# A four-layer kernel: the opening work of layer 0 as one program by chunks, layer 1's small products in four lanes, and clears moved

## The chip, the cores and the metric

The kernel runs on one core of a Trainium2 chip. The metric is the device time of one execution in microseconds; lower is better. The core has five engines with a program each: PE (TensorE, matrix products), DVE (VectorE), ACT (ScalarE), POOL (GpSimd) and SP (SyncE, which here only starts transfers). They meet through semaphores. PE's clock is granted at one of two levels, 1.2 or 2.4 GHz; a profile gives the granted level as a share of full speed.

## The reference

An activation `x` of 2 x 1024 tokens with 256 features goes through four residual layers, each a "conditioning" step and a feed-forward step. The change touches the first conditioning step and layer 1.

```python
# layer 0, conditioning: a demodulated product, w scaled per batch by the condition y
w1 = weight * y                        # per batch, with y / sqrt(256)
out = x @ (w1 / sqrt(sum(w1 ** 2) + 1e-8))
# layer 1, conditioning: attention with a query that is shared by all rows of a batch
q, k, v = x @ Wq.T, x @ Wk.T, x @ Wv.T          # 16 heads of 16
a = (Wt @ cond) . q                             # one weight per head and row
qmod = einsum('bhs,bhse->bhe', a, q)
scores = where(mask, qmod . k / sqrt(e), min); o = softmax(scores) @ v; out = o @ Wo.T
# layer 1, feed-forward: 16 experts' q, k, v and output projections,
# each weighted per token by a gating softmax rw; causal attention; out = sum_e rw_e * (ao @ o_proj_e)
```

Since the query of layer 1 does not depend on the row, all rows of a batch get the same attention result wherever all rows of `mask` are alike. Then the feed-forward part too is one row per batch, which is added to all 1024 tokens. The kernel tests this at run time and has a short branch for it, which the inputs take.

## The kernel before

Tokens are kept in SBUF as `xtok` (128 partitions x 16 tiles x 256) and, turned, as features `fx`/`fc` (128 x 2 halves x 2048 tokens). Both lie in one large tile, `sb_big` in the profile, as does `acc`. PE turns a block by a product with `ident`. The program is a row of *blocks*: in each, every engine has its own list, and the next block begins when all five have finished. After a group of blocks come two barriers of all engines and the release of semaphores (`with_own_semaphores`, line 2565).

Layer 0 opens with four blocks. `stage_load` (lines 105 to 162) loads `x` in one transfer of 2 MB, the condition, biases and router weights; ACT then waits for all of them and starts the clears of the scratch table `sorted_in` (39 tiles of 128 rows, 5.11 MB, three transfers), which only layer 2 reads. `stage_to_features` (L173, L181, L187) turns `x` in 32 transposes. `stage_l0_cond` loads its weight (L229), squares and folds it on DVE (L237, L240), gets the norm (L264), and does 16 products of 128x128 by 128x512 (L273), which DVE scales out of PSUM (L252). `stage_to_tokens` turns the result back in 32 transposes (L198, L206, L212). `half_l0` follows: router, shared expert, 32 routed experts whose weights are streamed by SP, results added. Its first PE rows are L298.

Layer 1, on this input, has four blocks. `stage_l1_project` (lines 1836 to 1940) loads the mask and the five weights, takes the query of every token (L1871, 16 products), copies it out (L1898), multiplies it by a block-diagonal condition (L1880) and sums over tokens on DVE (L1923), which gives `qmod` and then `U` (L1890). DVE meanwhile compares the mask's 8 tiles with its first row, one compare and one sum per tile (L1907, L1909). The count `differ` decides the branch. `stage_l1_same_rows` scores both batches in 16 output rows (L2428), softmax, a weighted sum of tokens (L2442), three small products; then a block `stage_l1_gating` with its own loads; then a block with the 16 experts' `v` projection (L2523: 32 products with two columns), output projection (L2529: 32 more), and the addition of the row to `fx` (L2553) and `xtok` (L2558). Layer 2's first rows follow.

Every fp32 product shows as two records in the profile, a transpose as one.

## Time and profile before

| | |
|---|---|
| median of 3 runs | 1822.16 us (1815.49 to 1824.17) |
| profiled execution | 1827.07 us, of it 1825.3 us span |
| mean granted PE clock | 0.905 |
| PE, DVE, ACT, POOL busy | 84%, 56%, 36%, 23% |
| span to the first row of `half_l0` on PE | 60.35 us |
| layer 1, first DVE row to layer 2's first ACT row | 371.93 to 497.84 us |

The span is cut below into the stages that the change touches and the rest. A profiled execution is one sample; its time lies a little above the highest of the three timed runs.

### The profile page before, as it was taken

How to read it: one execution, taken by the hardware profiler on the slowest of the kernel's cores; microseconds unless marked ns; L12 is line 12 of the kernel's file. 1: busy time of each engine (PE TensorE's matmuls, PEld its weight loads, DVE VectorE, ACT ScalarE, POOL GpSimd, SP SyncE). 2: the span in 40 equal slices, each digit the busy share in tenths (PEclk: the TensorE clock that was granted, in tenths of full speed). 3: DMA queues.
4: the chain of work that ended last, by engine and by line, in shares of the span. 5: the costliest groups of instructions: out<-in, count | busy, mean ns of one | idle time of the engine just before them, and what ended most of it. 6: DMA issues, size and time to landing. Idle time of an engine off the chain costs nothing. (4 is left out here: it accounts for less than half of the span.)

```text
span 1825.3 us, 26214 instructions
## 1 busy us (share of the span) xinstructions
PE 1533.0 (84%) x8442; PEld 1164.3 (64%) x8442; DVE 1013.2 (56%) x1801; ACT 661.3 (36%) x981; POOL 428.0 (23%) x364
## 2 busy tenths in 40 slices
PE   3788878866689999879799999999988699848993
PEld 2553323733668778768688888888776577725662
DVE  2737767452263435473577777776546133536675
ACT  1337767211032333242455555554323133211110
POOL 0412222000034241001033334342003334023321
PEclk9989989886579999989899999999997699959996
DMA  6328981213031334024022221300303232245733
GB/s 200 137 93 331 364 310 58 84 55 93 23 137 62 103 101 150 1 81 162 3 90 99 94 97 57 134 28 14 133 1 130 101 99 79 95 142 203 265 109 107
DMA packets 82585, 211.11 MB, mean 116 GB/s; under 512 B 10561, under 2 KB 57426, under 8 KB 74258
## 3 DMA queue, kind: packets, MB, share of 16 engines
q1 hardware_dynamic: 61568, 160.98, 24.8%
q0 software_dynamic: 15840, 43.27, 7.0%
q10 hardware_dynamic: 5042, 5.11, 0.8%
q8 instruction: 78, 1.28, 0.3%
q14 instruction: 57, 0.47, 0.1%
HBM read 164.90 MB, written 44.43 MB: 115 GB/s over the span
## 5 line engine op out<-in xcount | busy, mean ns | idle before, releaser
L593 POOL DMA_INDIRECT results<-sb_big,sb_s_out_row x63 | 132.8, 2108 | 465.1 <-ACT sb_big L824 303.1
L898 DVE TENSOR_TENSOR sb_h_split<-sb_big,sb_h_split 128x2048 fp32r<-128x2048 f32 x78 | 178.5, 2290 | 87.9 <-ACT sb_h_split L893 87.9
L893 ACT CAST sb_h_split<-sb_big 128x2048 fp32r x78 | 146.6, 1903 | 41.9 <-issue 40.6
L789 PE MATMUL ps<-sb_big,sb_e_hT 128*128 x624 | 141.0, 379 | 1.1 <-DVE sb_e_hT L942 1.1
L282 PE MATMUL ps<-sb_h_split 128*128 128x512 f32 x312 | 133.6, 428 | 9.6 <-DVE sb_h_split L917 6.8
L1031 DVE COPY sb_g_space<-sb_big 128x1024 f32 x168 | 108.4, 699 | 47.0 <-DMA sb_big<-in_l_routed 24.9
L1031 ACT COPY sb_g_space<-sb_big 128x1024 f32 x120 | 118.7, 1050 | 41.7 <-DMA sb_big<-in_l_routed 32.4
L1421 POOL DMA_INDIRECT sorted_in<-sb_big,sb_p_slots x64 | 70.6, 1104 | 260.6 <-DVE sb_p_slots L1247 216.8
L789 PEld LDWEIGHTS ps<-sb_big,sb_e_hT 128*128 128x128 f32 x624 | 118.2, 190 | 18.5 <-issue 1.3
L282 PE MATMUL ps<-sb_g_split,sb_g_ws 128*128 128x512 f32 x256 | 109.6, 428 | 23.3 <-DVE sb_g_product L461 15.7
L284 PE MATMUL ps<-sb_h_split 128*128 128x512 f32 x312 | 124.1, 398 | 0.0
L283 PE MATMUL ps<-sb_h_split 128*128 128x512 f32 x312 | 123.9, 397 | 0.0
L1069 PE MATMUL ps<-sb_g_space,sb_e_rT 128*32 128x512 f32 x768 | 99.9, 640 | 18.3 <-ACT sb_g_space L1031 8.5
L555 POOL DMA_INDIRECT results<-sb_big,sb_p_out_row x78 | 77.6, 995 | 145.3 <-DVE sb_big L704 144.6
L283 PE MATMUL ps<-sb_g_split,sb_g_ws 128*128 128x512 f32 x256 | 107.3, 419 | 0.0
L284 PE MATMUL ps<-sb_g_split,sb_g_ws 128*128 128x512 f32 x256 | 106.5, 416 | 0.0
L282 PE MATMUL ps<-sb_g_ws,sb_g_split 128*128 128x256 f32 x256 | 79.6, 311 | 26.1 <-DVE sb_g_split L467 18.5
L582 POOL DMA_INDIRECT sb_big<-by_token,sb_s_in_row x63 | 64.5, 1025 | 153.0 <-DVE sb_s_out_row L1294 134.4
L436 ACT ACTIVATE sb_g_sg<-ps 128x512 f32<-128x512 f32 x64 | 38.2, 598 | 157.0 <-PE ps L284 108.8
L636 PE MATMUL ps<-sb_big,sb_x_rT 128*128 x312 | 87.5, 403 | 4.1 <-ACT sb_x_rT L681 4.0
L461 DVE TENSOR_TENSOR sb_g_product<-sb_g_sg,ps 128x512 f32<-128x512 f32 x64 | 43.8, 685 | 70.8 <-ACT sb_g_sg L436 54.2
L656 PE MATMUL ps<-sb_big,sb_x_hT 128*128 x312 | 82.1, 386 | 0.0
(416 smaller groups left out, 3318.6 us busy)
## 6 DMA issues: line engine op xcount, KB each, us to landing
sb_big<-in_l_routed SPq DMA_DIRECT2D x32, 1024.0 KB
sb_big<-in_l2f_routed SPq DMA_DIRECT2D x8, 3072.0 KB, 11.1
sb_e_wring<-in_l_experts SPq DMA_DIRECT2D x16, 1408.0 KB
sb_big<-in_l_routed SPq DMA_DIRECT2D x32, 512.0 KB
sb_big<-results SPq DMA_DIRECT2D x32, 512.0 KB, 7.4
sb_big<-sorted_in SPq DMA_DIRECT2D x18, 512.0 KB
by_token<-sb_big SPq DMA_DIRECT2D x12, 512.0 KB, 3.6
sorted_in<-sb_big ACTq DMA_DIRECT2D x2, 2048.0 KB
```

The lines of the kernel that those rows point to most:

```text
L282: pe.matmul(to, w[0], x[0], start=start, stop=False)
L283: pe.matmul(to, w[0], x[1], start=False, stop=False)
L284: return pe.matmul(to, w[1], x[0], start=False, stop=stop)
L555: pool.indirect_dma_start(out=results, out_offset=bass.IndirectOffsetOnAxis(ap=places.out_row[:, j:j + 1], axis=0), in_=self.tile(j), in_o ...
L593: pool.indirect_dma_start(out=results, out_offset=bass.IndirectOffsetOnAxis(ap=places.out_row[:, j:j + 1], axis=0), in_=self.tile(j), in_o ...
L636: last = pe.matmul(psum[:, j % 2, 0:self.NF * P], self.rT[:, j % 2, k * P:(k + 1) * P], self.w[:, e, k * self.NF * P:(k + 1) * self.NF * P ...
L656: last = pe.matmul(psum[:, 2 + j % 2, 0:D], self.hT[:, j % 2, f * P:(f + 1) * P], self.w[:, e, lo:lo + D].rearrange("p s n -> p (s n)"), s ...
L789: last = pe.matmul(psum[:, 7, 0:D], self.hT[:, f // TPC, f % TPC * P:(f % TPC + 1) * P], self.weight(place, 2 * KD * self.F + f * D, D), s ...
L893: act.copy(self.own[part][:, 0, :], self.raw(e, part)).then_inc(self.own_high[part], 1)
L898: dve.tensor_tensor(self.own[part][:, 1, :], self.raw(e, part), self.own[part][:, 0, :], ALU.subtract).then_inc(self.own_low[part], 1)
L1031: last = copy(self.own[part][:, g, :], here.rearrange("p s n -> p (s n)"))
L1069: last = pe.matmul(psum[g * W:(g + 1) * W, 2 * part + u % 2, :], self.rT[:, r % 2, k, g * W:(g + 1) * W], self.own[part][:, g, lo:lo + FU] ...
```

## The change

The layer-0 opening becomes one block, `layer0_front`. `x` comes in four chunks of 512 tokens with a semaphore each, behind the condition and the weight. PE turns chunk 0 and 1, then for each chunk does the product, turns the chunk two ahead, and turns back the one before; DVE and ACT copy and scale in the same order. ACT clears only row 0 of `by_token`.

Layer 1's weights (now six, with a second layout of `Wq`) and the mask, viewed as 32-bit words, are loaded by SP at the end of `half_l0` into free parts of `sb_big`. `stage_l1_project` does not form the query of every token any more: it folds condition and `Wq` into 32 columns `V`, multiplies all tokens by them with four column groups of PE side by side (*lanes*: chunk g goes to partitions 32g to 32g+31), turns the result, and takes the weighted sum of tokens in the same manner. DVE compares the mask in three instructions over 2048 words per partition. SP clears `sorted_in` in this block, out of a zero tile that POOL makes; layer 2's POOL waits for it (`swept`). `stage_l1_same_rows` is one block with its loads at its head, the gating inside it, and the two expert projections in lanes (8 products of 32x512, 16 of 32x256). ACT takes half of the addition to `fx`. The branch for masks that differ is nearly unchanged.

```diff
-        def stage_load():
...
-                    sp.dma_start(xtok, a["x"].rearrange("(i p) d -> p i d", p=P)).then_inc(loaded, 16)
...
-                    act.wait_ge(loaded, 16 * 9)
-                    for lo in range(0, SLOT_TILES2, NT):
-                        hi = min(SLOT_TILES2, lo + NT)
-                        act.dma_start(sorted_in[lo * P:hi * P, :].rearrange("(i p) d -> p i d", p=P),
-                                      acc[:, 0:hi - lo, :]).then_inc(zeroed, 16)
-                    act.dma_start(by_token[0:1, :], acc[0:1, 0, :]).then_inc(zeroed, 16)
...
+        def layer0_front():
...
+                        sp.dma_start(condT[:], a["condT"]).then_inc(cond_in, 16)
+                        sp.dma_start(w[:], a["l0_cond_w"]).then_inc(w_in, 16)
+                        for c in range(NCH):
+                            sp.dma_start(xtok[:, c * TPC:(c + 1) * TPC, :],
+                                         a["x"][c * CH:(c + 1) * CH, :].rearrange("(i p) d -> p i d", p=P)).then_inc(x_in[c], 16)
+                        sp.dma_start(wr0[:], a["l0_gate"]).then_inc(loaded, 16)
+                        sp.dma_start(wbuf[:], unit_data["l0"]).then_inc(unit_in["l0"], 16)
...
+                        turn(0)
+                        pe.wait_ge(folded, 1)
+                        turn(1)
+                        for c in range(NCH):
+                            product(c)
+                            if c + 2 < NCH:
+                                turn(c + 2)
+                            if c >= 1:
+                                turn_back(c - 1)
+                        turn_back(NCH - 1)
...
+                        act.wait_ge(cleared, 1)
+                        act.dma_start(by_token[0:1, :], acc[0:1, 0, :]).then_inc(zeroed, 16)
...
+                        for c in range(NCH):
+                            scale(c)
+                            if c + 2 < NCH:
+                                to_features(c + 2)
+                            if c >= 1:
+                                to_tokens(c - 1)
+                        to_tokens(NCH - 1)
...
+                        sp.dma_start(l1_weights, a["l1_w"]).then_inc(l1_in, 16)
+                        sp.dma_start(l1_words[:, 0:TPB, :], a["mask_words"].rearrange("(i p) s -> p i s", p=P)
+                                     ).then_inc(l1_mask, 16)
+                        sp.dma_start(l1_words[:, TPB, :], a["mask_words"][0, :].partition_broadcast(P)).then_inc(l1_mask, 16)
...
-                        pool.wait_ge(zeroed, 16 * (1 + -(-SLOT_TILES2 // NT)))
+                        pool.wait_ge(zeroed, 16)
...
+                        if n == 2:
+                            pool.wait_ge(swept, 16 * 3)
...
-            stage_to_features("a0", xtok, fx)
-            stage_l0_cond()
-            stage_to_tokens("b0", fc, ctok)
+            layer0_front()
...
+        def in_lanes(pe, to, w, bank):
+
+            for k in range(KD):
+                for g in range(NCH):
+                    last = pe.matmul(psum[g * EQ:(g + 1) * EQ, bank, :], w[:, k, :], fx[:, k, g * CH:(g + 1) * CH],
+                                     start=(k == 0), stop=(k == KD - 1))
+            last.then_inc(to, 1)
...
+        def lanes_times_rows(pe, to, turned, bank):
+
+            for q in range(TPC):
+                for g in range(NCH):
+                    last = pe.matmul(psum[g * EQ:(g + 1) * EQ, bank, 0:D], turned[:, q, g * EQ:(g + 1) * EQ],
+                                     xtok[:, g * TPC + q, :], start=(q == 0), stop=(q == TPC - 1))
+            last.then_inc(to, 1)
...
+                        for lo in range(0, SLOT_TILES2, NT):
+                            n = min(SLOT_TILES2 - lo, NT)
+                            sp.dma_start(sorted_in[lo * P:(lo + n) * P, :].rearrange("(i p) d -> p i d", p=P),
+                                         zero[:].unsqueeze(1).to_broadcast([P, n, D])).then_inc(swept, 16)
...
+                        pe.wait_ge(vc, 1)
+                        in_lanes(pe, ad, V, 0)
+                        pe.wait_ge(ac, 1)
+                        turn_lanes(pe, atd, lanes, TPC, 1)
+                        pe.wait_ge(atc, 1)
+                        lanes_times_rows(pe, rd, aT, 2)
+                        pe.wait_ge(rc, 1)
+                        turn_lanes(pe, rtd, r, KD, 3)
...
-                            dve.tensor_tensor(ne[:], m8[:, i, :], m1[:], ALU.not_equal).then_inc(counted, 1)
-                            dve.wait_ge(counted, 2 * i + 1)
-                            dve.tensor_reduce(cnt[:, i:i + 1], ne[:], AX_X, ALU.add).then_inc(counted, 1)
...
+                    for g in range(NCH):
+                        sp.dma_start(m1[g * EQ:(g + 1) * EQ, :],
+                                     a["mask"][0, g % 2 * CH:(g % 2 + 1) * CH].partition_broadcast(EQ)).then_inc(masked, 16)
+                    sp.dma_start(simc[:, :, 0:E], a["l1_sim"]).then_inc(simmed, 16)
+                    sp.dma_start(gb[:], a["l1_gates"].partition_broadcast(P)).then_inc(simmed, 16)
+                    for k in range(KD):
+                        sp.dma_start(wv[:, :, k, :], a["l1_qkv"][:, :, k, 2 * H1:3 * H1]).then_inc(wloaded, 16)
+                    sp.dma_start(wo[:], a["l1_o"]).then_inc(wloaded, 16)
...
-            stage_l1_gating(rw, shared=cb)
...
-                        for e in range(E1):
-                            for k in range(KD):
-                                last = pe.matmul(psum[:, 0, e * B:(e + 1) * B], wv[:, e, k, :], c[:, k, :],
-                                                 start=(k == 0), stop=(k == KD - 1))
-                        last.then_inc(vd, 1)
...
+                    pe.wait_ge(wloaded, 48)
+                    for k in range(KD):
+                        for g in range(4):
+                            last = pe.matmul(psum[g * EQ:(g + 1) * EQ, 6, :], c32[:, k, :], wv[:, 4 * g:4 * g + 4, k, :],
+                                             start=(k == 0), stop=(k == KD - 1))
+                    last.then_inc(vd, 1)
+                    pe.wait_ge(vsd, 1)
+                    pe.matmul(psum[:, 5, 256:256 + B], vs[:], sel[:], start=True, stop=True).then_inc(vtd, 1)
...
+                    pe.wait_ge(avd, 2)
+                    for n in range(4):
+                        for g in range(4):
+                            last = pe.matmul(psum[g * EQ:(g + 1) * EQ, 7, 0:D], av[:, 4 * g + n, :], wo[:, 4 * g + n, :],
+                                             start=(n == 0), stop=(n == 3))
+                    last.then_inc(outd, 1)
...
+                    act.wait_ge(simmed, 32)
+                    act.activation(gb[:], gb[:], ACT.Sigmoid).then_inc(rooted, 1)
+                    act.wait_ge(maxd, 1)
+                    act.activation(pr[:], pr[:], ACT.Exp, bias=mx[:, 0:1], accum_out=sums[:, 0:1]).then_inc(expd, 1)
...
-        with_own_semaphores(stage_load)
...
```

PE's rows at the start of the program, before: `sb_big` holds `x` and its turned copy, `sb_l0c_wb` the folded weights; a branch row is the step into the next block.

```order
L173 MATMUL ps<-sb_ident,sb_big 128x128 x32
L167 UNCONDITIONAL_BRANCH
L259 UNCONDITIONAL_BRANCH
L264 MATMUL ps<-sb_l0c_ys,sb_l0c_w 128x2 x4
L273 MATMUL ps<-sb_big,sb_l0c_wb 128x512 x16
L226 UNCONDITIONAL_BRANCH
L192 UNCONDITIONAL_BRANCH
L198 MATMUL ps<-sb_ident,sb_big 128x128 x32
```

The same place in the changed program (L172 turns a chunk, L184 is the product, L196 turns it back):

```order
L203 MATMUL ps<-sb_l0c_ys,sb_l0c_w 128x2 x4
L172 MATMUL ps<-sb_ident,sb_big 128x128 x16
L184 MATMUL ps<-sb_big,sb_l0c_wb 128x512 x4
L172 MATMUL ps<-sb_ident,sb_big 128x128 x8
L184 MATMUL ps<-sb_big,sb_l0c_wb 128x512 x4
L172 MATMUL ps<-sb_ident,sb_big 128x128 x8
L196 MATMUL ps<-sb_ident,sb_big 128x128 x8
L184 MATMUL ps<-sb_big,sb_l0c_wb 128x512 x4
L196 MATMUL ps<-sb_ident,sb_big 128x128 x8
L184 MATMUL ps<-sb_big,sb_l0c_wb 128x512 x4
L196 MATMUL ps<-sb_ident,sb_big 128x128 x16
```

The 80 products and transposes and the norm are the same in number; the three steps between blocks are gone, and the norm stands first.

PE's rows in layer 1 before, first of the projection block, then of the last block of the short branch:

```order
L1863 MATMUL ps<-sb_condT,sb_l_w 128x2 x4
L1871 MATMUL ps<-sb_big,sb_l_w 128x512 x16
L1880 MATMUL ps<-sb_big,sb_l_bd 128x512 x8
L1884 MATMUL ps<-sb_l1p_cnt,sb_ones 1x8
L1890 MATMUL ps<-sb_l_qm,sb_l_w 128x16 x8
...
L2523 MATMUL ps<-sb_f_c,sb_f_wbuf 128x2 x32
L2529 MATMUL ps<-sb_f_av,sb_f_wbuf 128x2 x32
L2535 MATMUL ps<-sb_ident,sb_f_rowb 128x128 x4
```

And in the changed program (`V`, `aT`, `rb` lead to the query, `wv` and `wo` are the experts' weights):

```order
L1935 MATMUL ps<-sb_condT,sb_big 128x2 x4
L1941 MATMUL ps<-sb_l_tpm,sb_big 128x32 x4
L1867 MATMUL ps<-sb_big,sb_l_V 32x512 x8
L1882 MATMUL ps<-sb_ident,sb_l_lanes 128x128 x4
L1875 MATMUL ps<-sb_big,sb_l_aT 32x256 x16
L1882 MATMUL ps<-sb_ident,sb_l_r 128x128 x2
L1956 MATMUL ps<-sb_l_rb,sb_big 128x32 x4
L1963 MATMUL ps<-sb_l_qm,sb_big 128x32 x4
...
L2545 MATMUL ps<-sb_f_wv,sb_f_c 32x512 x8
L2549 MATMUL ps<-sb_f_sel,sb_f_vs 128x2
L2553 MATMUL ps<-sb_f_wo,sb_f_av 32x256 x16
L2558 MATMUL ps<-sb_f_sel,sb_f_rows 128x2 x2
```

The 24 wide products of the projection become 8 of a quarter of the width in output rows plus 16 short ones, and 64 two-column products of the experts become 24 in lanes.

## Rows read from the trace of the kernel before

**Rows 1.** The first line of the page.
```profile
span 1825.3 us, 26214 instructions
```

**Rows 2.** Busy time by stage: opening, layer 1's four blocks, the rest.
```profile
core 0: us, PE busy (x) PEld busy (x) DVE busy (x) ACT busy (x) POOL busy (x), PEclk, DMA share, GB/s
0.00:60.30 60.30, 27.60 (x104) 17.15 (x104) 18.17 (x32) 7.46 (x11) 2.25 (x15) 0.94 0.47 152
...
371.80:413.70 41.90, 27.38 (x74) 13.55 (x74) 27.41 (x46) 4.92 (x9) 0.71 (x3) 0.79 0.17 60
413.70:444.00 30.30, 25.81 (x92) 11.45 (x92) 6.16 (x18) 3.53 (x5) 0.07 (x1) 0.73 0.44 139
444.00:459.90 15.90, 4.45 (x20) 4.34 (x20) 6.02 (x32) 4.60 (x7) 0.00 (x0) 0.50 0.02 3
459.90:497.50 37.60, 28.72 (x132) 28.17 (x132) 8.38 (x12) 0.00 (x0) 0.00 (x0) 0.50 0.00 0
```

**Rows 3.** Timeline of the opening: start, duration, instruction, idle before it.
```profile
11.11 11.33 ACTq L127 DMA_DIRECT2D sorted_in<-sb_big  x3
...
25.78 5.81 PE L173 MATMUL ps<-sb_ident,sb_big 128*128 128x128 f32 x32 [25.78 <-PEq L2567]
...
35.01 0.69 DVE L237 TENSOR_TENSOR sb_l0c_w<-sb_l0c_w 128x512 f32<-128x512 f32 x1 [2.13 <-DMA sb_l0c_w<-in_l_cond_w]
...
37.61 17.05 PE L273 MATMUL ps<-sb_big,sb_l0c_wb 128*128 128x512 f32 x32 [0.80 <-DVE sb_l0c_d L246]
...
55.75 3.69 PE L198 MATMUL ps<-sb_ident,sb_big 128*128 128x128 f32 x32 [1.09 <-PEq L226]
...
60.35 1.92 PE L298 MATMUL ps<-sb_big,sb_wr 128*32 128x512 f32 x16 [0.92 <-PEq L191]
```

**Rows 4.** Transfers issued in the opening: KB, and us from issue to landing.
```profile
sb_big<-in_x SPq DMA_DIRECT2D x1, 2048.0 KB, 8.4
```

**Rows 5.** DVE's groups in the opening: busy us, mean ns, idle before.
```profile
L252 DVE TENSOR_SCALAR sb_big<-ps,sb_l0c_d 128x512 f32<-128x512 f32 x8 | 6.0, 751 | 12.0 <-PE ps L273 12.0
...
L206 DVE COPY sb_big<-ps 128x512 f32<-128x512 f32 x4 | 2.8, 692 | 1.5 <-PE ps L198 1.5
```

**Rows 6.** Granted clock during L273 (columns of rows 2).
```profile
42.00:44.00 2.00, 2.00 (x4) 0.90 (x3) 0.23 (x1) 0.00 (x0) 0.00 (x0) 0.55 0.00 0
44.00:46.00 2.00, 2.00 (x6) 0.85 (x5) 0.75 (x1) 0.00 (x0) 0.00 (x0) 1.00 0.00 0
```

**Rows 7.** Granted clock in layer 1 (columns of rows 2).
```profile
371.80:389.00 17.20, 7.17 (x15) 4.08 (x16) 10.06 (x10) 0.59 (x1) 0.69 (x2) 0.51 0.41 145
389.00:411.00 22.00, 19.70 (x57) 9.06 (x56) 16.92 (x34) 4.10 (x7) 0.00 (x0) 1.00 0.00 1
```

**Rows 8.** Costliest groups of the projection block (columns of rows 5).
```profile
L1871 PE MATMUL ps<-sb_big,sb_l_w 128*128 128x512 f32 x32 | 16.5, 679 | 0.0
...
L1909 DVE TENSOR_REDUCE sb_l1p_cnt<-sb_l1p_ne 128x1 f32<-128x1024 f32 x8 | 9.8, 1220 | 0.3
...
L1863 PE MATMUL ps<-sb_condT,sb_l_w 128*128 128x2 f32 x8 | 1.9, 356 | 12.2 <-DMA sb_l_w<-in_l_w 12.2
```

**Rows 9.** Timeline of the gating block (columns of rows 3).
```profile
447.94 1.28 ACT L2141 ACT_TABLE_LOAD   x1
...
453.67 0.19 DVE L2165 TENSOR_TENSOR sb_g1s_L<-sb_g1s_L,sb_g1s_ns 128x32 f32<-128x32 f32 x1
453.90 0.19 DVE L2166 TENSOR_TENSOR sb_g1s_L<-sb_g1s_L,sb_g1s_gb 128x32 f32<-128x32 f32 x1
```

**Rows 10.** Transfers issued in layer 1 (columns of rows 4).
```profile
sb_g1s_gb<-in_l_gates SPq DMA_DIRECT2D x1, 8.0 KB, 3.1
```

**Rows 11.** Costliest groups of the last block of layer 1 (columns of rows 5).
```profile
L2529 PE MATMUL ps<-sb_f_av,sb_f_wbuf 128*128 128x2 f32 x64 | 13.8, 352 | 0.9 <-DVE sb_f_av L2546 0.9
...
L2558 DVE TENSOR_TENSOR sb_big<-sb_big,ps 128x2048 f32<-128x2048 f32 x2 | 4.5, 2280 | 0.0
```

**Rows 12.** Timeline of PE at the start of layer 2 (columns of rows 3).
```profile
501.56 3.41 PE L298 MATMUL ps<-sb_big,sb_wr2c 128*32 128x512 f32 x16
```

More of the change, by code:

```diff
@@ new lines, in lanes_times_rows, with turn_lanes @@
+        def lanes_times_rows(pe, to, turned, bank):
+            for q in range(TPC):
+                for g in range(NCH):
+                    last = pe.matmul(psum[g * EQ:(g + 1) * EQ, bank, 0:D], turned[:, q, g * EQ:(g + 1) * EQ],
+                                     xtok[:, g * TPC + q, :], start=(q == 0), stop=(q == TPC - 1))
+            last.then_inc(to, 1)
+        def turn_lanes(pe, to, lanes, n, bank):
+            for q in range(n):
+                last = pe.transpose(psum[:, bank, q * P:(q + 1) * P], lanes[:, q * P:(q + 1) * P], ident[:])
+            last.then_inc(to, 1)
@@ L1883, in _ @@
[L1883 to L1891 removed]
+                        pe.wait_ge(tpmd, 2)
@@ new lines, in _ @@
+                        for d in range(KD):
+                            for o in range(KD):
+                                last = pe.matmul(psum[:, 6, d * BH:(d + 1) * BH], w6[:, WQT, o, d * P:(d + 1) * P],
+                                                 tpm[:, o, :, :].rearrange("p b h -> p (b h)"),
+                                                 start=(o == 0), stop=(o == KD - 1))
+                        last.then_inc(vd, 1)
+                        pe.wait_ge(vc, 1)
+                        in_lanes(pe, ad, V, 0)
@@ L1892, in _ @@
+                        last.then_inc(qd, 1)
+                        pe.wait_ge(qmd, 2)
+                        for d in range(KD):
+                            for o in range(KD):
+                                last = pe.matmul(psum[:, 5, d * BH:(d + 1) * BH], w6[:, WK, o, d * P:(d + 1) * P],
+                                                 qm[:, o, :, :].rearrange("p b h -> p (b h)"),
+                                                 start=(o == 0), stop=(o == KD - 1))
                         last.then_inc(ud, 1)
+                        pe.wait_ge(counted, 1)
@@ L1894, in _ @@
+                        pe.matmul(psum[0:1, 7, 64:65], ones[:, 0:1], cnt[:], start=True, stop=True).then_inc(flagd, 1)
                     @block.scalar
                     def _(act):
-                        for n in range(8):
-                            act.wait_ge(qd, n + 1)
-                            act.copy(q[:, n // NCH, n % NCH * CH:(n % NCH + 1) * CH], psum[:, n % 4, :]).then_inc(qc, 1)
+                        act.wait_ge(ad, 1)
+                        act.copy(lanes[:], psum[:, 0, :]).then_inc(ac, 1)
@@ new lines, in stage_l1_same_rows @@
+            E, BH = E1, B * HEADS
+            wv = sb("f1_wv", [P, E, KD, H1], on=own)
+            wo = sb("f1_wo", [P, E, D], on=own)
+            m1 = sb("f1_m1", [P, CH], U8, on=own)
+            lim = sb("f1_lim", [P, CH], on=own)
+            pr = sb("f1_pr", [P, CH], on=own)
+            pT = sb("f1_pT", [P, TPC, P], on=own)
+            mx, sums = (sb("f1_" + n, [P, 1], on=own) for n in ("mx", "sums"))
+            spread = sb("f1_spread", [P, 2, P], on=own)
+            peak, total, share, tmp2 = (sb("f1_" + n, [P, B, 2, HEADS], on=own) for n in ("peak", "total", "share", "tmp2"))
@@ L2570, in layer1 @@
             with ExitStack() as own:
[L2571 removed]
+                w6 = l1_weights
                 U = sb("l1_U", [P, KD, B, HEADS], on=own)
```

804 lines of the change are left out of this document (420 added, 384 removed).

## The prediction, made before the changed kernel ran

> **What bounds the kernel now.** I read the page first: the span is 1825.3 us [rows 1], and its profiled execution took 1827.1 us. The chain that ended last covers only the last 1% of the span, so it says nothing about the places of this change. I then cut the span at the borders of the edited blocks and took the busy time of each stretch [rows 2]. The reader is to see that no engine is full in any of them. The opening takes 60.3 us and PE, the busiest engine, works 27.6 of it. Layer 1 runs from 371.8 to 497.5, in pieces of 41.9, 30.3, 15.9 and 37.6 us, 125.7 in all. DMA is idle in most of it (share 0.17, 0.44, 0.02, 0.00). These stretches are dependent chains, so what counts is the length of the chain, and an instruction off it is free.
>
> The timeline of the opening [rows 3] shows the chain. ACT issues three clears from 11.11 for 11.33 us, and PE's first transpose is at 25.78, only after them, although `x` landed 8.4 us after its issue at the start [rows 4]. Then come 5.81 us of transposes, 2.13 us of waiting for a weight that had no reason to come so late, 17.05 us of products, 3.69 us of transposes and, at 60.35, the router. The clears are on the path because the block ends only when ACT has issued them.
>
> In layer 1 PE waits 12.2 us for the weights before its first small product, then works 16.5 us on the query of every token, while DVE sums the mask in 8 pieces of 1.22 us beside as many compares [rows 8]. In the last block two sets of 64 records with two columns each take 13.8 us apiece, 27.6 of 37.6 us (one of them in [rows 11]): these pay for loading 128x128 weights, not for columns. The clock matters: at 0.51 of full speed in the first 17.2 us of the layer and 1.00 in the next 22 [rows 7], then 0.50 in the last two pieces [rows 2].
>
> **The opening, part by part.** The work on PE is the same; its place changes. Removed are the wait for clears and the steps between blocks. The condition and weight are first in SP's queue. I take 4 us for the weight, as its load made DVE wait about 2 us when issued alone [rows 3]. A 2 MB `x` took 8.4 us to land [rows 4]; if about 2 us of that is fixed, a quarter costs 1.6 and chunk 0 lands near 5.5, chunk 3 near 10. With no fixed part a quarter is 2.1 us and nothing below changes by more than 1 us. The norm is done at 5.7. Two chunks of transposes at the slow pace of the first ones (5.81 us for 32, 0.18 each) give 8.7. The 16 products I price as now, 17.05 us, which includes a slow start: the records before 44 us ran at a granted 0.55, those after at 1.00 [rows 6]. Between them stand 16 forward transposes and 16 backward ones at 0.115 each (3.69 for 32), 3.7 us. DVE's load per chunk is two scalings of 0.75 and two copies of 0.69 [rows 5], 2.9 us against 4 to 5 us of PE, so it is covered; with PE free it would be 11.5 us in all. At the end stand out one scaling, the copies of chunk 2 and 3 and the last 8 transposes, 0.75 + 0.69 + 0.92 + 0.69, plus 0.5 for a small DVE instruction and the step: 3.6. Sum 8.7 + 17.05 + 3.7 + 3.6 = 33.0 against 60.3, **27.3 us less**. Bounds: with a full clock throughout 3 us less; with the half clock throughout the products are 16 x 1.71 = 27.4 and the 56 later transposes 0.06 each dearer, so 13.7 more.
>
> What follows in layer 0 starts from the same state and keeps its length; its streamed weights are asked for at its own start, so they shift along. The shared expert's weights come behind `x`, 1.5 MB at the pace of `x`, near 16 us, 17 before use.
>
> **The prefetch.** SP issues 2.7 MB more behind the result loads at the end of layer 0. At the pace of `x` (2 MB in 8.4) they need 11 us, about 335 to 345, with some 25 us of product work left before layer 1. Cost nothing; without that cover up to 11 us.
>
> **Layer 1, projections.** After a first small product the engines take turns, PE's bursts being under 4 us. Now the clock came up only after some 6 us of continuous products and fell again in the waits [rows 7], so I price all at half clock: four small products in 1.9 us [rows 8], eight 32x512 in lanes in 3.4 us [rows 12] (1.92 at full clock [rows 3]), and sixteen 32x256 as the same columns. The chain: condition 1.9, masking 0.6, `V` 1.9 and copy 0.2, lanes 3.4, copy 0.6, four transposes 0.8, copy 0.7, lanes 3.4, copy, two transposes and DVE's halves 1.6, query 1.9, scaling 0.4, `U` 1.9 or beside it DVE's sum of 2048 words at 2 x 1.22 = 2.4, copies and flag 0.5. That is 20.3 us. DVE's word compare (2.3 us, as L2558's 2.28 for 2048 elements [rows 11]) lies behind the first lanes and its copies, the conversion (at most the same) behind the second. With the step to the next block, 1.7 us as now, 22.0 against 41.9: **19.9 less**. The clears are asked for at its head by SP: issue 11.3 us [rows 3], landing at most 5.11/2.1 x 8.4 = 20.4 us; that ends inside the block, and their reader is in layer 2. If they ran on, the next block's mask and gate loads would queue behind.
>
> **Layer 1, the rest.** Six small transfers go out first; the last is issued at 2.2 us and lands 3.1 later [rows 10], then sigmoid 0.2 and a table load of 1.28 [rows 9]: exp can start at 6.8, later than the scores (3.5) and their maximum (4.9). This wait is new, about 2 us; behind it on ACT stand exp and all that leads to the weighted sum, so PE and DVE wait too. Then exp 0.8, transposes and copy 1.5, spreading of maxima 1.1, lanes 3.4, copy, turn and weighting 1.6: 15.2. Three small products with their DVE parts, 2.3, 2.7 and 1.9: 22.1. Gating, 31 instructions at 0.23 from start to start [rows 9] and two trips to ACT, 8.2, which hides the first expert product (3.4 in place of 13.8): 30.3. Two DVE passes over 512, a tiny product and `av`, 2.4; second expert product 3.4 in place of 13.8; row 1.5; `fx` halved between DVE and ACT 1.4; `xtok` 4.5 as now: 43.5. With a step of 1.3, 44.8 against 83.8: **39.0 less**. The experts' weights land about 17 us in, needed at 22.
>
> Sum: 27.3 + 19.9 + 39.0 = 86.2 us. The profiled execution would take 1827.1 - 86.2 = 1740.9; it lay 4.9 above the median, so the median becomes **1736 us**.
>
> On the four lanes: 16 records took 3.41 us [rows 12], where at 0.85 a record they would be 13.7 in full width, a gain of 4.0. The Trainium skill (TensorE: Matmul & The Clock Gate, Measured speedup vs the span model) gives 3.07 for four row tiles and less than 3 for three column tiles. By that figure, an estimate, each of the five lane products would be 4.5 us, of them four on the path, and the time 1740. The row is of this very shape, so it decides.
>
> On the table switch: the load takes 1.28 us and the sequence needs nothing more in this trace [rows 9]. The Trainium skill (ScalarE: Activation LUTs, What ACT_TABLE_LOAD costs) adds a drain and gives 2.66 us for a switch; the sum would be 1737.
>
> **The rivals.**
> Half clock all through the opening (0.13). Chunks mix transposes into the products, and PE's first 32 transposes ran at 0.18 us, the later ones at 0.115. For it: the opening starts from idle and its bursts are broken. Against: the products alone are 3.4 us long with hardly a gap. By the bound above it costs 13.7 us: 1750 us. The same skill page (Part 4: PE-mode transpose) says that transposes do not count as work that raises the clock, which speaks for this case; it hangs on no row here.
> Clock up in layer 1 (0.10). Four small products 1.05 instead of 1.9, lanes 1.9 instead of 3.4: 13 us less, 1723. Against: every burst is under 4 us.
> Underpriced hand-overs or the clears colliding (0.14). If each of some 40 hand-overs cost 0.3 us more, or the clears took twice 15 us and pushed the mask loads 8 us back, the time is 1748.
> The opening gives nothing (0.03): if layer 0's streamed weights, not its start, set its end. They are issued at its own start, so this needs a limit that no row shows; 1763.
> Slower than before (0.02). PE leaves layer 1 at half clock, as now, where it recovered in 17 us of layer 2. If it stayed there, each microsecond of full PE work costs one more. It decides above 86 + 9 = 95 us of such work; layer 2 has over 200. One mechanism, and nothing in the trace shows it: 1832.
>
> **How the numbers follow.** My own sum has 0.58, with its own range 1727 to 1746. The rivals at 1750, 1748 and 1723 lie close by and are taken in, so the range is **1719 to 1758**; outside are the last two and tails. Half a per cent, 9 us, is about what a measurement tells from no change here (three runs lay 8.7 apart). Faster 0.96, same 0.02, slower 0.02.
>
> **What will show it.** PE's router rows should start near 33 us, the first transpose near 6, with at most 0.6 us between products and turns after the first. Layer 1 should be 67 us long from its first DVE row to layer 2, the projection block 20 and the other 43.5; mask loads should not be behind clears; lanes should take 3.4 us each at a granted 0.50. Wrong would be: a clock at 0.50 past 20 us, a clear still running at 394, an exp that starts later than 7 us into its block, or a stretch of layer 0 that grew by what the opening lost.

## The result, and the profile after

The changed kernel takes **1734.22 us** (median of four executions, 1731.22 to 1737.56); the kernel before, run beside it on the same chip, 1823.16 (1815.49 to 1827.36). The ratio is 0.9518, with a 95% interval from 0.9488 to 0.9547: 89 us less, where 86 were forecast. The profiled execution is the slowest of the four, 1737.56 us with a span of 1735.8.

Busy time by stage of the changed kernel, columns as in [rows 2]: opening, rest of layer 0, layer 1's two blocks, the step behind them, all the rest.

```profile
0.00:30.70 30.70, 24.32 (x105) 16.05 (x105) 14.92 (x32) 6.20 (x11) 2.25 (x15) 1.00 0.41 131
30.70:340.45 309.75, 249.48 (x2156) 137.68 (x2156) 191.42 (x310) 174.98 (x246) 70.65 (x64) 0.94 0.59 212
340.45:362.30 21.85, 15.35 (x88) 9.15 (x88) 8.32 (x17) 1.17 (x3) 0.96 (x4) 0.58 0.66 235
362.30:405.99 43.69, 24.60 (x142) 11.75 (x142) 20.65 (x72) 9.67 (x15) 0.60 (x2) 0.62 0.32 99
405.99:411.29 5.30, 0.00 (x0) 0.00 (x0) 0.00 (x0) 1.57 (x3) 0.00 (x0) 0.50 0.51 167
411.29:1735.80 1324.51, 1168.66 (x5864) 951.89 (x5864) 755.65 (x1351) 463.51 (x702) 351.67 (x282) 0.92 0.29 99
```

Against [rows 2] the opening is 29.7 us shorter (router's first row at 30.70, before at 60.35 [rows 3]), the projection block 20.0 (21.9 for 41.9), and the rest of layer 1 is one block of 43.7 us where three took 83.8 (to 497.5, and so with 1.3 us of the step behind them), with a step of 5.3 behind it. PE's share in the opening rose from 27.6 of 60.3 to 24.3 of 30.7. All this lies in the first 411 us.

PE's timeline in the opening after. The norm (L203) comes first; chunks then follow without a gap until the last turn:

```profile
4.80 1.87 PE L203 MATMUL ps<-sb_l0c_ys,sb_l0c_w 128*128 128x2 f32 x8 [4.80 <-DVE sb_l0c_w L252]
6.52 3.42 PE L172 MATMUL ps<-sb_ident,sb_big 128*128 128x128 f32 x16
9.78 3.60 PE L184 MATMUL ps<-sb_big,sb_l0c_wb 128*128 128x512 f32 x8
13.21 1.04 PE L172 MATMUL ps<-sb_ident,sb_big 128*128 128x128 f32 x8
...
28.71 1.06 PE L196 MATMUL ps<-sb_ident,sb_big 128*128 128x128 f32 x8 [0.66 <-DVE sb_big L275]
30.70 1.92 PE L335 MATMUL ps<-sb_big,sb_wr 128*32 128x512 f32 x16 [0.93 <-PEq L118]
```

PE's timeline in layer 1 after:

```profile
340.49 1.69 PE L1935 MATMUL ps<-sb_condT,sb_big 128*128 128x2 f32 x8 [2.42 <-PEq L2697]
...
345.05 3.64 PE L1867 MATMUL ps<-sb_big,sb_l_V 128*32 128x512 f32 x16 [0.32 <-DVE sb_l_V L1989]
...
384.43 3.64 PE L2545 MATMUL ps<-sb_f_wv,sb_f_c 128*32 128x512 f32 x16
393.97 0.59 PE L2549 MATMUL ps<-sb_f_sel,sb_f_vs 128*128 128x2 f32 x2 [5.90 <-DVE sb_f_vs L2676]
395.23 3.61 PE L2553 MATMUL ps<-sb_f_wo,sb_f_av 128*32 128x256 f32 x32 [0.67 <-DVE sb_f_av L2680]
...
411.29 0.41 PE L1415 MATMUL ps<-sb_condT,sb_wr2c 128*32 128x1 f32 x16 [10.37 <-issue]
```

Most of these products run at the half clock, as priced: the mean granted clock is 0.58 in the first block and 0.62 in the second. Where two experts' products of 13.8 us stood [rows 11], two of 3.64 and 3.61 stand, and behind the first PE still waits 5.90 us for the gating on DVE.

The new wait stands on ACT where it was forecast. Its timeline after:

```profile
367.83 0.22 ACT L2566 ACTIVATE sb_f_gb<-sb_f_gb 128x16 f32<-128x16 f32 x1 [4.46 <-DMA sb_f_gb<-in_l_gates]
368.06 1.28 ACT L2568 ACT_TABLE_LOAD   x1
369.36 0.72 ACT L2568 ACTIVATE sb_f_pr<-sb_f_pr,sb_f_mx 128x512 f32<-128x512 f32 x1
```

The exp's maximum was ready at 367.18 and the exp starts at 369.36, 7.06 us into its block: 2.2 us of waiting for the gates' load, the sigmoid and the table.

### The profile page after: what moved, and what is told of

Same layout as the page of the kernel before. It is cut to its first block and busy times, and to the rows that moved or that the text cites. A ratio compares the mean times of both kernels' runs of the same rounds, so it can differ in the third digit from the quotient of the medians.

```text
span 1735.8 us, 25954 instructions
## 1 busy us (share of the span) xinstructions
PE 1482.4 (85%) x8354; PEld 1126.5 (65%) x8354; DVE 991.0 (57%) x1782; ACT 657.1 (38%) x977; POOL 426.1 (25%) x366
## 5 line engine op out<-in xcount | busy, mean ns | idle before, releaser
L1106 PE MATMUL ps<-sb_g_space,sb_e_rT 128*32 128x512 f32 x768 | 95.7, 616 | 21.2 <-ACT sb_g_space L1068 9.6
L319 PE MATMUL ps<-sb_g_ws,sb_g_split 128*128 128x256 f32 x256 | 78.5, 307 | 25.2 <-DVE sb_g_split L504 14.5
## 6 DMA issues: line engine op xcount, KB each, us to landing
sb_big<-in_l2f_routed SPq DMA_DIRECT2D x8, 3072.0 KB, 10.5
```

The source lines that it names most:

```text
L319: pe.matmul(to, w[0], x[0], start=start, stop=False)
L1106: last = pe.matmul(psum[g * W:(g + 1) * W, 2 * part + u % 2, :], self.rT[:, r % 2, k, g * W:(g + 1) * W], self.own[part][:, g, lo:lo + FU] ...
```

## The experiments

Twelve kernels ran. Two yardsticks serve for all, and each profile is one sample. "Rows" is the start of the router's first row on PE, 30.70 in the changed kernel. "Layer 1" runs from the end of layer 0's last turn on PE to layer 2's first row on PE: 338.07 to 411.29, **73.2 us**, in the changed kernel. Code that no run altered varies by itself: with the same opening, "rows" lay at 30.7 to 32.4 in nine profiles, and the part after layer 1 lasted 1318.9 to 1325.3 us in the same nine. So medians some 5 us apart say little, and the trace decides. Layer 1 varies too. In the runs 1, 3 and 4 below its products are those of the changed kernel, and it lasted 75.6, 75.0 and 75.2 us, not 73.2: small products that took 1.08 and 1.05 us in the changed kernel's profile took 1.91 and 1.87 there, about twice as long. A difference from 73.2 is therefore uncertain by some 2 us, and where that matters the rows of the edited place are given.

**1. The old opening without its clears.** It separates the two halves of the opening's gain.

```diff
-            layer0_front()
+            stage_to_features("a0", xtok, fx)
+            stage_l0_cond()
+            stage_to_tokens("b0", fc, ctok)
...
+        with_own_semaphores(stage_load)
```

`stage_load` is as before, but without the three transfers into `sorted_in`.

> The changed kernel with the old four-block opening put back, but without the clears of the sorted rows in it (they stay in layer 1). Theory 1 (the clears' issue alone held the old opening for about 13.4 us of the 29.7 gained, from the clears' issue of 11.3 us and the wait behind it; work by chunks gives the other 16.3): the router's rows start at about 30.7 + 16.3 = 47 us and the time is 1734 + 16 = 1750. Rival 1 (nearly all of the gain was the clears; chunks only move work about): 1737 or less. Rival 2 (the clears ran hidden behind the loads, chunks gave it all): 1764.

Measured: 1754.17 us, ratio 0.9619 [0.9593, 0.9645]. PE's timeline of this run:

```profile
12.09 6.42 PE L356 MATMUL ps<-sb_ident,sb_big 128*128 128x128 f32 x32 [12.09 <-PEq L2845]
22.69 1.87 PE L447 MATMUL ps<-sb_l0c_ys,sb_l0c_w 128*128 128x2 f32 x8 [4.18 <-DVE sb_l0c_w L420]
25.36 16.95 PE L456 MATMUL ps<-sb_big,sb_l0c_wb 128*128 128x512 f32 x32 [0.80 <-DVE sb_l0c_d L429]
43.40 3.69 PE L381 MATMUL ps<-sb_ident,sb_big 128*128 128x128 f32 x32 [1.09 <-PEq L409]
48.01 1.49 PE L481 MATMUL ps<-sb_big,sb_wr 128*32 128x512 f32 x12 [0.92 <-PEq L374]
```

Rows at 48.01: the clears' place was worth 60.35 - 48.01 = **12.3 us**, the new order of the work 48.01 - 30.70 = **17.3 us**. Theory 1 holds, both rivals fall. The 17.3 are not the chunks' alone: PE's wait of 4.18 us before the norm, the steps between blocks and the slow first products went at the same time, and no run parts these.

**2. The new opening alone**, in the kernel before, with the clears on SyncE behind the opening's loads.

> The kernel before with the new opening alone: layer 1 as it was, and the clears issued by SyncE at the end of the opening's own list. Theory 1 (the parts add up, and the clears cost nothing behind the loads): 1823 less 29.7 less about 1.6 of layer 0 = 1792, router's rows from 30.7 us. Rival 1 (the clears on SyncE's queue hold the opening's end or its x loads): the rows start later than 31, by up to the clears' issue of 8 to 11 us, and the time is 1793 to 1803. Rival 2 (part of the 29.7 is only got together with layer 1's change): above 1800 with the rows at 30.7.

Measured: 1793.02 us, ratio 0.9834 [0.9808, 0.9860]; rows at 32.11. That is 29 us less than the kernel before, and its opening is 28.2 shorter (32.11 for 60.35). Both lie at the near edge of rival 1, but rows at 32.11 are within the 30.7 to 32.4 of the profiles without these clears, so it isn't borne out. The parts add up: the opening's gain needs nothing from layer 1.

**3. and 4. Where the clears stand.** In the changed kernel they go back into the opening, once on SyncE behind its loads, once on ScalarE ahead of its copies.

```diff
...
+                        sp.wait_ge(swiped, 1)
+                        for lo in range(0, SLOT_TILES2, NT):
+                            n = min(SLOT_TILES2 - lo, NT)
+                            sp.dma_start(sorted_in[lo * P:(lo + n) * P, :].rearrange("(i p) d -> p i d", p=P),
+                                         zero_rows[:].unsqueeze(1).to_broadcast([P, n, D])).then_inc(swept, 16)
                         sp.wait_ge(loaded, 16 * 7)
+                        sp.wait_ge(swept, 16 * 3)
...
```

> The changed kernel with the clears back in the opening, behind SyncE's loads. Theory 1 (what matters is only that the clears are off the queue that the products wait for; their place is free): 1734, within 2. Rival 1 (the clears' writes slow x and the weights' landings): the first rows of the router later than 30.7 by 1 to 5, 1736 to 1739. Rival 2 (their place in layer 1 cost something there): up to 2 faster, seen in a shorter projection block than 21.9.

> The changed kernel with the clears issued by ScalarE at the head of its list in the opening, ahead of its copies. Theory 1 (an issue on the engine that copies holds those copies): ScalarE's first copy, which now follows the transposes at about 8 to 9 us, comes after the issue of 8 to 11 us that starts at about 1, so 2 to 5 us late, and the opening ends as much later: 1736 to 1739. Rival 1 (the queue drains them in the background, hidden): 1734. Rival 2 (as costly as in the kernel before): 1745 or more.

On SyncE: 1737.71 us, ratio 0.9520 [0.9488, 0.9553], rows at 31.72. No difference from the changed kernel that can be told; PE's first products took 4.42 us in it, where the changed kernel's took 3.60, and in other profiles of the same opening they took 3.60 to 4.91, so this is most likely not the clears' doing. By its number and its rows this run would also fit rival 1; against that rival stands that `x` was asked for in 2.08 us in both and that the first transpose started at 6.39, in the changed kernel at 6.52. Rival 2 finds nothing either: the block in layer 1 that lost the clears was not shorter.

On ScalarE: 1754.64 us, ratio 0.9614 [0.9584, 0.9645], rows at 46.26, 14.5 late against SyncE's. ScalarE's timeline shows why:

```profile
1.15 13.67 ACTq L226 DMA_DIRECT2D sorted_in<-sb_l0c_zero  x3
14.87 6.52 ACTq L229 DMA_DIRECT2D by_token<-sb_big  x1
21.41 1.28 ACT L231 ACT_TABLE_LOAD   x1 [21.41 <-issue]
22.71 0.21 ACT L231 ACTIVATE sb_l0c_d<-sb_l0c_d 128x4 f32<-128x4 f32 x1
22.82 1.06 ACT L235 COPY sb_big<-ps 128x512 f32<-128x512 f32 x2
```

Rival 2 holds: I had counted the clears' issue of 11 us and left out the small transfer behind them. That one took 0.48 us in the changed kernel and 6.52 here, in line behind the clears, and the square root and all copies stand behind it. PE waited 8.78 us for the copy at 22.82. The clears also slowed the loads beside them: SyncE took 5.56 us to ask for `x` in place of 2.08, and the first transpose started at 9.94, but PE had turned both chunks by 14.75, well ahead of that copy. The two runs differ in the engine and in the place (ahead of the loads and copies, or behind the loads); the clears at the head of SyncE's list were not tried.

**5. No prefetch.** Layer 1's weights and the mask's words are loaded at the head of the projection block by the same three instructions.

> The changed kernel with layer 1's weights and the mask's words loaded at the head of the projection block, as before, and not in layer 0. Theory 1 (the weights' load stands ahead of everything in the block): the block grows from 21.9 by the load's issue and landing of 9 to 10.5 us less the start that it had anyway, so 1734 + 9 = 1743. Rival 1 (the half clock or the waits of the block hide part): 1738. Rival 2 (it gives nothing in layer 0 either way but also frees transfers there, .35 to .20 of the queue's share): layer 0 shorter by about 1, 1742.

Measured: 1742.59 us, ratio 0.9542 [0.9512, 0.9573]; layer 1 is 79.4 us, 6.2 more. The three loads stand ahead of the clears in SyncE's list. PE's timeline:

```profile
346.96 1.87 PE L1935 MATMUL ps<-sb_condT,sb_big 128*128 128x2 f32 x8 [8.81 <-DMA sb_big<-in_l_w]
```

8.81 us of waiting where the step to the block costs 2.42 anyway: the prefetch is worth **6.4 us**. I had expected 9, taking the landing times of 10.5 us that these transfers have behind layer 0's result loads; on an idle queue the weights landed 6.4 us after their issue. Theory 1's mechanism holds with a smaller price.

**6. The mask compared in bytes.** The 16 instructions of before, at the head of VectorE's list, in place of the three on words.

```diff
...
+                        dve.wait_ge(mloaded, 32)
+                        for i in range(TPB):
+                            if i:
+                                dve.wait_ge(counted, 2 * i)
+                            dve.tensor_tensor(ne[:], m8[:, i, :], m1[:], ALU.not_equal).then_inc(counted, 1)
+                            dve.wait_ge(counted, 2 * i + 1)
+                            dve.tensor_reduce(cnt[:, i:i + 1], ne[:], AX_X, ALU.add).then_inc(counted, 1)
                         dve.wait_ge(tpd, 1)
...
```

> The changed kernel with the mask compared as before by 16 instructions on bytes at the head of VectorE's list, and the rest of layer 1 new. Theory 1 (the count of about 16 instructions, eight pairs of some 1.6 us, stands ahead of VectorE's small copies that each product now waits for): the first product's copy comes about 13 us late, block 35, time 1747. Rival 1 (it is hidden behind the lanes' products as the one comparison is): 1736 or less. Rival 2 (only the flag comes late, at the block's end): 1738 to 1742.

Measured: 1762.48 us, ratio 0.9644 [0.9609, 0.9680]; layer 1 is 97.9 us, **24.7 more**, about twice what theory 1 expected. VectorE's groups between the block's start and its first copy:

```profile
L1990 DVE TENSOR_TENSOR sb_l1p_ne<-sb_l1p_m 128x1024 f32<-128x1024 uint8 x8 | 9.8, 1225 | 7.0 <-DMA sb_l1p_m<-in_mask 6.8
L1992 DVE TENSOR_REDUCE sb_l1p_cnt<-sb_l1p_ne 128x1 f32<-128x1024 f32 x8 | 9.8, 1220 | 0.3
```

Each pair costs 2.5 us, not 1.6, and the bytes' load adds 6.8 of waiting: 26.4, and PE's second product waited 25.66 for VectorE. The words, by contrast, are loaded in layer 0, cost 2.28, 1.22 and 2.28 us, and lie beside lanes and copies. In the kernel before this same compare lay beside 16.5 us of products [rows 8]; it ended at 398.8 there, and the last of those products at 400.0. With them gone it would be the bound of the block. The short chain and a compare off its path are one change. The run alters size and place together; 16 small instructions spread between the copies were not tried.

**7. and 8. The experts' products without lanes.** The v product, then the output product, as 32 separate products with two columns again.

```diff
...
-                    for n in range(4):
-                        for g in range(4):
-                            last = pe.matmul(psum[g * EQ:(g + 1) * EQ, 7, 0:D], av[:, 4 * g + n, :], wo[:, 4 * g + n, :],
-                                             start=(n == 0), stop=(n == 3))
+                    for f in range(KD):
+                        for e in range(E):
+                            last = pe.matmul(psum[:, 7, f * B:(f + 1) * B], wo[:, e, f * P:(f + 1) * P], av[:, e, 0:B],
+                                             start=(e == 0), stop=(e == E - 1))
...
```

> The changed kernel with the v product of the block of equal rows as 32 separate products again, without lanes. Theory 1 (its 13.8 us at half clock start at 384.4 beside the gating chain that ends at 392.2; about 6 us stick out, less some 2 us of lane sums on VectorE and TensorE that it doesn't need): 1734 + 4 = 1738. Rival 1 (hidden behind the gating): 1732 to 1734. Rival 2 (the busier TensorE comes to full clock by itself, product 7 us): 1732.

> The changed kernel with the output product of the block of equal rows as 32 separate products again, with the old broadcast and transposes behind it. Theory 1 (32 products of about 0.42 at half clock, 13.5, for 3.6, everything waits for it; the copy of rows and the products behind it, 2.2, against a broadcast and transposes of 2.7): 1734 + 10 = 1744. Rival 1 (the clock is full by then, as in the kernel before, where its output product took 4.5): 1734 to 1736. Which of the two holds tells how much of the lanes' gain is the lanes' own.

The v product: 1739.03 us, ratio 0.9526 [0.9506, 0.9545], layer 1 78.2 us, 5.0 more. The output product: 1746.33 us, ratio 0.9571 [0.9548, 0.9594], layer 1 84.2 us, 11.0 more. PE's timeline of the first:

```profile
388.10 13.79 PE L2545 MATMUL ps<-sb_f_c,sb_f_wv 128*128 128x2 f32 x64
402.88 3.64 PE L2551 MATMUL ps<-sb_f_wo,sb_f_av 128*32 128x256 f32 x32 [0.99 <-DVE sb_f_av L2671]
```

And of the second:

```profile
394.37 13.81 PE L2553 MATMUL ps<-sb_f_av,sb_f_wo 128*128 128x2 f32 x64 [0.67 <-DVE sb_f_av L2677]
```

From the start of the v product to that of the output product are 14.8 us, with lanes 10.8 (384.43 to 395.23; 10.8 also in run 1). So these lanes save 4.0 us, because the gating hides the rest; the same lanes in the output product, which nothing hides, save 13.81 - 3.61 = 10.2. Theory 1 holds in both. The second expectation's rival rests on a wrong figure: in the kernel before the output product took 13.8 us [rows 11], at a granted 0.50, and not 4.5.

**9. and 10. TensorE's waits filled.** 83 products of 128 by 128 (the expectation's 74 is a miscount) into an unused place, from layer 0's last turns to layer 1's end, each set sized to the wait that it stands ahead of; then the same with transposes of as much time.

```diff
+        def keep(pe, n, bank):
+            for i in range(n):
+                pe.matmul(psum[:, bank, 384:512], ones[:], ident[:], start=True, stop=True)
...
+                        keep(pe, 3, 5)
                         pe.wait_ge(ac, 1)
```

> The changed kernel with TensorE's waits from the last turns of layer 0 to the end of layer 1 filled with 74 products of 128 by 128 into an unused place of PSUM. Theory 1 (the half clock between 340 and 412 is what an often waiting TensorE gets; with its waits filled it keeps full clock): granted clock above 0.9 there, lanes' products 1.9 in place of 3.6, the two blocks shorter by 8 to 12: 1722 to 1727. Rival 1 (the clock stays half: small or narrow operations don't hold it): each wait is overrun by up to 0.4, 1737 to 1742. Rival 2 (clock full, but the fillers overrun the waits as much as it gains): 1732 to 1735.

> The same as the run with filling products, with transposes of as much time as fillers (5 for each 3 products). Theory 1 (a transpose holds the clock as a product does; in the opening products were at full clock behind 16 transposes): as the run with products, clock above 0.9, 1722 to 1728. Rival 1 (only products count, as the Trainium skill has it, in TensorE: Matmul & The Clock Gate): clock about 0.5 as without fillers, 1736 to 1742.

With products: 1727.60 us, ratio 0.9467 [0.9437, 0.9497], layer 1 67.1 us, 6.2 less than in the changed kernel. With transposes: 1728.82 us, ratio 0.9475 [0.9449, 0.9500], layer 1 65.0 us, 8.2 less. Windows of the run with products:

```profile
344.00:348.00 4.00, 4.00 (x20) 1.20 (x19) 2.42 (x2) 0.00 (x0) 0.00 (x0) 0.50 1.09 386
348.00:361.00 13.00, 9.95 (x88) 7.72 (x84) 5.28 (x10) 1.25 (x3) 0.09 (x2) 0.89 0.65 231
361.00:364.00 3.00, 2.92 (x16) 0.61 (x16) 0.00 (x0) 0.99 (x1) 0.52 (x2) 0.54 0.09 22
364.00:380.00 16.00, 13.32 (x119) 10.70 (x116) 6.46 (x29) 4.23 (x7) 0.00 (x0) 1.00 0.86 265
380.00:384.00 4.00, 3.79 (x20) 0.97 (x20) 2.86 (x17) 1.59 (x3) 0.00 (x0) 0.60 0.01 4
384.00:395.00 11.00, 10.26 (x96) 8.53 (x96) 6.42 (x25) 1.48 (x3) 0.00 (x0) 0.99 0.00 0
```

And of the run with transposes:

```profile
357.00:360.50 3.50, 3.50 (x16) 0.57 (x16) 0.00 (x0) 0.86 (x1) 0.39 (x1) 0.50 0.09 23
360.50:375.00 14.50, 12.06 (x108) 9.24 (x104) 6.46 (x29) 4.23 (x7) 0.00 (x0) 0.96 0.94 290
375.00:380.00 5.00, 5.00 (x25) 1.98 (x25) 2.78 (x16) 1.59 (x3) 0.00 (x0) 0.52 0.02 7
380.00:391.00 11.00, 10.15 (x88) 8.15 (x88) 6.41 (x25) 1.41 (x3) 0.00 (x0) 0.91 0.00 0
```

The seventh number is the granted clock. In the long stretches of chained work it is now 0.89 to 1.00 with either filler, and the 32x256 lanes took 1.93 us in place of 3.61. The changed kernel had 0.56 from 340.45 to 356, 0.50 from 362.3 to 378 and 0.65 from 382.5 to 405, with short stretches of 0.93 and 0.88 between. The rival of the second run falls with it: with transposes as fillers the clock stayed up as with products. The Trainium skill (TensorE: Matmul & The Clock Gate, Part 4: PE-mode transpose) says that they don't count; this trace disagrees, with 0.96 between 360.5 and 375 where the same work without fillers (362.3 to 378) had 0.50. Still the clock was at 0.50 to 0.60 in the lanes of 32x512, the first and the later one of the second block too, though TensorE was busy nearly all the time (4.00 of 4.00 us in the first): ahead of them stand small products of 2 to 32 columns, or the step between blocks. Why it fell there no run shows. So the gain in layer 1 is 6 to 8 us against the changed kernel's own profile, up to 11 against the 75.6 of run 1, and not 13 throughout. The 2 us between the two fillers are within what layer 1 varies by.

**11. The gates early.** The sigmoid, an idle exp that brings the table in, and the loads of mask lanes, similarities and gates move to the projection block.

```diff
                         act.copy(r[:], psum[:, 2, 0:D]).then_inc(rc, 1)
+                        act.wait_ge(simmed, 32)
+                        act.activation(gb[:], gb[:], ACT.Sigmoid)
+                        act.activation(idle[:], ones[0:1, 0:1], ACT.Exp)
```

> The changed kernel with the sigmoid of the gates, an idle exp behind it, and the loads of the mask's lanes, the similarities and the gates moved from the block of equal rows to the projection block. Theory 1 (the exp at 7.06 us into the block waits 2.2 us for the sigmoid and the table's load, nothing else is late there): exp at 4.9, time less 2.2: 1732. Rival 1 (the table is loaded anew at the exp in any case): less 0.9 or nothing. Rival 2 (another wait takes its place, the spread products' or the mask's): less 0 to 1, 1733 to 1734.

Measured: 1732.49 us, ratio 0.9496 [0.9464, 0.9527]; layer 1 71.8 us, 1.5 less, which is within its own variation. ScalarE's timeline has both table loads in the block before and none at the exp:

```profile
358.16 1.28 ACT L1984 ACT_TABLE_LOAD   x1
359.45 0.22 ACT L1984 ACTIVATE sb_f_gb<-sb_f_gb 128x16 f32<-128x16 f32 x1
359.67 1.28 ACT L1985 ACT_TABLE_LOAD   x1
...
371.21 0.72 ACT L2570 ACTIVATE sb_f_pr<-sb_f_pr,sb_f_mx 128x512 f32<-128x512 f32 x1 [10.04 <-DVEq L2593]
```

From the start of the scores' lanes to the transposes behind the exp are 5.4 us (366.64 to 372.08), in the changed kernel 7.8 (362.46 to 370.22), in the runs 1, 3 and 4 7.5 to 7.7: the wait of about 2.2 us is won. The time of the whole kernel can't tell 2 us, so this rests on the rows.

**12. Both together**: the filling products and the early gates.

> Filling products and the early gates together. Theory 1 (they add): 10 and 2.2, 1722; with the lanes' product faster the early exp is worth up to 4: 1720. Rival 1 (the fillers stay at half clock and cost): 1735 to 1740.

Measured: 1729.91 us, ratio 0.9476 [0.9451, 0.9500]; layer 1 64.1 us, 9.1 less than in the changed kernel and 3.0 less than with the fillers alone. From the scores' lanes to the transposes behind the exp are 6.6 us, with filling products alone 8.7, so the early gates are worth 2.1 here too: the two add in these rows (theory 1, which had put the sum at 12). The medians don't show it, 1729.91 against 1727.60 with products alone. The three versions with fillers are the fastest here, by their ratios 0.4 to 0.5% under the changed kernel, but their intervals touch its own. That they beat it rests on the shorter layer 1 in each trace, 64.1 to 67.1 us against 73.2 to 75.6.

**What was not run.** No run puts back the query of every token, or the three blocks of the rest of layer 1 with their steps. The prefetch (6.4 of the projection block's 20) and the experts' lanes (14.2 of the rest's 39) are priced by experiments; what is left in each, about 14 and 24 us, is read from the traces before and after.

## Why the prediction was right

**The opening** (27.3 forecast, 29.7 measured). The mechanism was right: clears off the path 12.3, the new order of the work 17.3. One term was mis-sized: "the 16 products I price as now, 17.05 us, which includes a slow start". They took 4 x 3.60 = 14.4. Against that the first products began at 9.78 where 8.7 was reckoned. The slow start belongs to the old order, where PE idles before its products; in the old opening without clears they took 16.95 again, at a granted 0.50 from 25 to 31 us. Here transposes stand right ahead of them. Other profiles of the same opening show up to 1.3 us of it. Behind an idle of 8.78 us, with the clears on ScalarE, the first products took 5.40. The rival of a half clock all through the opening does not hold: four of its products took 3.60 us, and at the half clock the prediction reckons 1.71 for each. The profile's own reading can't settle it: it is 1.00 from the start, though the norm took 1.87 us, while eight records of the same shape in layer 1 took 1.84 at a granted 0.50 (run 3) and 1.02 at 1.00 (run 9).

**The clears** (issue 11.3, inside the block). SyncE issued them from 340.79 for 7.83 us, where 11.3 was reckoned, and from 356 the DMA share is 0.01; the mask's loads are issued at 362.4. The half of that rival that rests on a collision falls. On SyncE they cost nothing that can be told in either place.

**The prefetch** (0, or up to 11 without cover). It cost layer 0 nothing that can be told: its remainder took 309.8 us, before 311.5, and from "rows" to the last turn it was 304.9 to 309.1 in eight profiles with it and 305.8 in the one without. It saves 6.4.

**The projections** (22.0 forecast, 21.9 measured). The small products took 1.69, 1.92, 1.08 and 1.92, lanes 3.64 and 3.36; PE's six waits for DVE and ACT up to the query 0.32 to 0.92. The half clock held, but for 2 us at 356 to 358, where it was 0.93. That the total fits to 0.1 us is luck: in five other profiles with the same products (runs 1, 3, 4, 7 and 8) the block lasted 23.5 to 23.8 us from its first product to the next block's, and 22.0 here (22.1 in run 5). The price of the compare (2.3) and that it lies behind the lanes were right; what it is worth I had not worked out, and the sixth run puts it at some 25 in this kernel (25.66 us of waiting where 0.63 is usual).

**The rest of layer 1** (block 43.5, then a step of 1.3; measured 43.7 and 5.3). Exp was forecast at 6.8 and came at 7.06, just past the 7 that was named as a sign of being wrong. The cause was the forecast's own, the gates' load, the sigmoid and the table; the maximum was ready at 4.88, as reckoned. The forecast's step ends at 497.5 [rows 2], but PE's first row lies later in both kernels: at 501.32 before, 5.1 us behind DVE's last row, and 5.3 behind it now. So 0.2 us was lost there. By the measure of the prediction, first DVE row to layer 2, the layer took 69.2 us to ACT's first row (340.54 to 409.72) and not 67: that row lies 3.7 us behind DVE's last one, before it lay 1.6 behind. Lanes: 13.8 us became 3.64 and 3.61 at the half clock, a gain of 3.8. By the Trainium skill's 3.07 for four row tiles (TensorE: Matmul & The Clock Gate, Measured speedup vs the span model), an estimate, they would have taken 4.5; the trace has less. The table load took 1.28 us and the exp began 0.02 behind it; the further drain that the Trainium skill gives (ScalarE: Activation LUTs, What ACT_TABLE_LOAD costs) is not in this trace.

**The clock in layer 1.** The rival at 1723 asked for a full clock there. It did not come by itself; with fillers 6 to 8 of its 13 us come, measured against the changed kernel's profile.

**The sum.** In the profiles the opening gave 29.7, layer 0's remainder 1.7 where nothing was forecast, the projections 20.0, the rest of layer 1 up to layer 2's first PE row 38.6, and what follows took 0.5 more: 89.5 us. No large error hides behind another; the largest is the 2.7 us of the opening's products.

## What to carry to other kernels

Before pricing a chain, ask for each engine what stands ahead of the small instruction that the others wait for: three clears ahead of ScalarE's small transfer and copies cost 14.5 us, behind SyncE's loads none that can be told, and sixteen instructions of 1.2 us for the compare cost about 25 once the products beside them were gone. When a dependent chain of short products runs at the half clock, filling TensorE's waits with idle products or transposes is cheap to try and gave at least 6 to 8 us of 73. Judge an edit of a few microseconds by the rows that it changes, since the untouched remainder varied by 6 and a layer with the same products by 2.4 from one profile to the next.

## What the hardware showed unexpectedly

- With transposes as fillers the granted clock was 0.89 to 0.96 over the waits, with products 0.89 to 1.00.
- With TensorE busy 4.00 of 4.00 us the granted clock was still 0.50, in lanes that followed small products.
- In the opening the granted clock reads 1.00 while the norm's eight records take 1.87 us, as such records do in layer 1 at 0.50 (1.84 in run 3), and while the first 16 transposes take 0.21 us each and later ones 0.13. What held them I did not test; the reading alone is no proof of a full clock there.
- A transfer of 1 KB took 0.48 us to issue on a free queue and 6.52 behind 5 MB of clears.
- Three clears took 11.33 us to issue on ScalarE in the kernel before, 13.67 there beside the loads, 9.11 on SyncE behind the opening's loads, and 7.83 on SyncE in layer 1.
